# Cross-attention with layer norm on one core: a V projection and a Q projection of the next batch trade steps, and one V projection of the last batch moves an iteration forward

## The chip, the cores and the metric

One Trainium2 chip, of which the kernel uses one core. The metric is device time in microseconds (us). The kernel before took 638.55 us (median of three runs, 637.2 to 639.08).

## The reference

Eight batches. For each, `x` (224 rows of 512) attends to `ctx` (750 rows of 512) with 16 heads of width 32, in float32:

```python
q = (x @ Wq.T + bq); k = (ctx @ Wk.T + bk); v = (ctx @ Wv.T + bv)      # split into 16 heads of 32
att = softmax(einsum('bhqd,bhkd->bhqk', q, k) / sqrt(32))
out = einsum('bhqk,bhkd->bhqd', att, v)                                # heads side by side again
out = x + (out @ Wo.T + bo)
out = (out - mean(out)) / sqrt(var(out) + 1e-05) * gamma + beta
```

All biases, gamma and beta are non-trivial.

## The kernel before, in words

**Tiles.** The queries are two halves of 112 rows, the keys six tiles of 125 (`KT`), the heads four groups of four (`UNITS`, `HG`). A unit is one group of heads of one batch, so there are 32. Projections and scores run in fp16 with each operand split in a high and a low part. A projection is therefore three products for each of four chunks of 512: twelve matmuls. K tasks (`("K", g, half)`) have 375 columns, Q tasks (`("Q", g)`) 224, V tasks (`("V", i)`) 512.

**Steps.** The program is unrolled over the eight batches. An iteration has 32 steps (`STEPS`), eight for each unit. In step s TensorE (PE) first computes the query-major scores of step s+1 (L626, one head, 112 queries, 750 keys), of which VectorE (DVE) takes the row maximum (L928). A step also has key-major score pieces of the unit before (L650), which ScalarE (ACT) exponentiates into `probsT` (L809); the table `PIECES_IN` says how many before, inside and behind the step's task. The third kind of work is the step's projection task (L610). A scores matmul of step s+1 waits until the row maximum of step s-1 is done, since two score banks alternate.

**Sums and visit.** GpSimd (POOL) sums the exponentials of each head over its keys: `pair_sums` (L1036) and two adds into `head_sums` (L1041, L1044). Heads 0 to 3 of a unit are summed at steps 4, 5 and 7 of one slot of eight steps, and at step 0 of the next. At step 2 of that slot (steps 2, 10, 18, 26) PE makes a visit for that unit: 48 matmuls `attend` (L666) and 8 matmuls `sum_keys` (L692), which wait for `head_sums`. ACT copies the result one step later (L817), DVE inverts it (L935, step 4), scales it (L940, step 5) and writes its low half (L950, step 7).

**Tasks.** `OWN` are tasks of this batch, `NEXT` of the next, `OUTPUT` the output projection of the batch before (steps 17 and 20). Two PSUM banks alternate between the tasks of slots' steps 0, 1, 2, 4, 5, 7, where step 2 is the visit. The task of a step may start when the task two uses before in that order is saved (`user_before`), and behind a visit when ACT has copied it. The saving happens one step later: of K and Q tasks ACT writes the high half, then DVE the low half (L885) after that step's row maximum; of a V task DVE alone copies the bank (L890), ahead of that step's row maximum. So K3 of step 31 (`("K", 3, 0)`) must be saved before Q2 of the next iteration's step 1 can start.

**Norm.** The output of the batch before is scaled with `gamma` on DVE (`times_gamma`, L915) at steps 26 and 29, behind the row maximum and the saving; `beta` is added on POOL (`plus_beta`, L1060) at steps 27 and 30. POOL's own order in the stretch is: head 3 (step 24), beta (27), head 0 (28), head 1 (29), beta (30), head 2 (31). Iteration 0 has no output of a batch before.

**DMA queue.** SyncE (SP) issues all loads, the transposes of the tokens, and `fill_stack`, which copies K and Q of a group into stacks with 16 DMAs. Its order at the end of an iteration: `fill(0)`, both stores, `fill(1)` (which waits for K1 and Q1), the load of `resid`; then the transposes of the next iteration. The second store waits for the second `plus_beta`.

**The last batches.** Iteration 6 leaves out the tasks that `LATE` names, and iteration 7 makes them itself, at the steps in `LATE` (`EARLY` is the rest of `NEXT`).

Of the kernel before, what the change touches and what calls it, by code (L numbers as in the profile page):

```python
# [15 lines left out]
def build(nc, x, ctx_tokens, Wq, bq, Wk, bk, Wv, bv, Wo, bo, gamma, beta, out):  # L16
# [49 lines left out]
    VISIT = 2  # L66
    OWN = {0: ("K", 2, 1), 1: ("Q", 2), 4: ("K", 3, 1), 5: ("V", 3), 7: ("V", 4), 8: ("Q", 3), 9: ("V", 5)}
    NEXT = {12: ("K", 0, 0), 13: ("K", 1, 0), 15: ("V", 0), 16: ("V", 1), 21: ("K", 0, 1), 23: ("K", 1, 1), 24: ("Q", 0),
            25: ("Q", 1), 28: ("V", 2), 29: ("K", 2, 0), 31: ("K", 3, 0)}
    SPLIT = {1: (("ctxT", 0),), 2: (("ctxT", 1), ("ctxT", 2)), 10: (("ctxT", 3), ("ctxT", 4), ("ctxT", 5)),  # L70
             18: (("xT", 0), ("xT", 1))}
    SPLIT_ORDER = [t for s in sorted(SPLIT) for t in SPLIT[s]]
# [3 lines left out]
                    ("xT", 0): ("Q", 3), ("xT", 1): ("Q", 3)}  # L76
    OUTPUT = {17: ("O", 0), 20: ("O", 1)}
    FIRST = {2: ("V", 2), 10: ("W", "o", 1), 17: ("W", "o", 2), 20: ("W", "o", 3)}
    LATE = {12: ("V", 0), 13: ("V", 1), 15: ("V", 2)}
    TASK_BANKS = 2  # L80
    IN_BANKS = (0, 1, 2, 4, 5, 7)
    VISIT_BANK = IN_BANKS.index(VISIT) % TASK_BANKS
    EARLY = {s: t for s, t in NEXT.items() if t not in LATE.values()}
    EARLY_V = [t[1] for t in NEXT.values() if t[0] == "V"]
# [35 lines left out]
    def tasks_of(b):  # L120

        known = isinstance(b, int)
        found = dict(OWN) if not known or b < B else {}
        found.update(NEXT if not known or b < LAST - 1 else EARLY if b == LAST - 1 else LATE if b == LAST else {})
        found.update(OUTPUT if not known or b > 0 else FIRST)
# [981 lines left out]
```

## Time and profile before

| | |
|---|---|
| median of three runs | 638.55 us |
| profiled execution | 640.04 us, of which 637.3 us are the span from first to last instruction |
| granted PE clock, mean | 0.994 |
| PE matmul | 611.6 us busy (96%) |
| DVE | 501.1 us (79%) |
| POOL | 468.0 us (73%) |
| ACT | 352.5 us (55%) |

A unit of the trace is a microsecond from the start of the span. PE's busy time takes each matmul with its whole length in the pipeline. Iterations 1 to 5 have the same length to a few hundredths, 74.0 us, so one of them (iteration 4, whose step 25 starts at 382.97) stands for all.

### The profile page before, as it was taken

Reading aid. Unit: us, or ns where it says so; the run is one execution under the profiler, and the core shown is the slowest. Engines: PE = TensorE matmul, PEld = TensorE weight load, DVE = VectorE, ACT = ScalarE, POOL = GpSimd, SP = SyncE. Lnnn points to the kernel's source line nnn. Section 1 sums busy time; section 2 is a strip of 40 time slices with the busy share of each in tenths; the row PEclk is TensorE's granted clock in tenths of the full one; section 3 lists DMA queues with packets and bytes.
Section 4 is the critical chain, followed back from the end, with each engine's and each line's share of the span. In section 5 each row is a group of like instructions: output and inputs, shape, how many; then the busy total and the mean of one; then the engine's idle time right before and its main releaser. Section 6 shows DMA issues by size and latency. Waiting matters only on the chain.

```text
span 637.3 us, 13655 instructions
## 1 busy us (share of the span) xinstructions
PE 611.6 (96%) x5217; PEld 425.4 (67%) x5217; DVE 501.1 (79%) x680; ACT 352.5 (55%) x673; POOL 468.0 (73%) x459
## 2 busy tenths in 40 slices
PE   8998999999999999999999999999999999899894
PEld 7766677766676676766677676766767666576542
DVE  4677787788797797887787887977878887757885
ACT  4514566556565465664665565664656656444661
POOL 9633677784987589784987759785897869775853
PEclk9999999999999999999999999999999999899998
DMA  9574532562245523754137532564237422421020
GB/s 304 186 183 126 133 78 72 133 145 70 65 110 142 129 63 89 151 127 125 38 86 167 143 77 62 115 147 118 69 88 169 96 62 51 107 69 25 2 59 29
DMA packets 95776, 67.02 MB, mean 105 GB/s; under 512 B 69780, under 2 KB 81760, under 8 KB 95712
## 3 DMA queue, kind: packets, MB, share of 16 engines
q1 hardware_dynamic: 95200, 65.41, 41.2%
q0 software_dynamic: 512, 0.75, 0.5%
q8 instruction: 41, 0.67, 0.4%
q14 instruction: 23, 0.19, 0.1%
HBM read 24.52 MB, written 3.67 MB: 44 GB/s over the span
## 4 chain that ended last, share of the span: by engine, by line
PE 69%; POOL 14%; DVE 12%; issue 3%; DMA 1%; ACT 1%; POOLq 0%; SPq 0%; DVEq 0%; ACTq 0%
PE ps_task L610 34%; PE ps_scores L626 10%; PE ps_scoresT L650 8%; PE ps_task L666 6%; POOL pair_sums L1036 6%; DVE top L928 4%; PE ps_task L564 4%; POOL head_sums L1041 3%; DVE token_parts L905 3%; POOL head_sums L1044 3%; PE ps_scores L610 2%; POOL rstd L1056 2%; PE ps_task L692 2%; DVE attn_sums L935 1%; DMA x_in<-in_x 1%
## 5 line engine op out<-in xcount | busy, mean ns | idle before, releaser
L809 ACT ACTIVATE probsT<-ps_scoresT 125x448 f32<-125x448 f32 x384 | 204.5, 544 | 154.2 <-PE ps_scoresT L650 148.4
L928 DVE TENSOR_REDUCE top<-ps_scores 112x1 f32<-112x750 f32 x256 | 234.2, 927 | 63.8 <-PE ps_scores L626 63.0
L1036 POOL TENSOR_TENSOR pair_sums<-probsT 125x672 f32<-125x672 f32 x122 | 197.8, 1621 | 72.3 <-ACT probsT L809 65.6
L650 PE MATMUL ps_scoresT<-stacks 100*125 100x224 f16 x768 | 135.8, 261 | 1.5 <-ACT probsT L809 1.2
L610 PE MATMUL ps_task<-wvT,ctxT 128*125 128x512 f16 x564 | 135.6, 379 | 0.1
L610 PE MATMUL ps_task<-ctxT,wkT 128*128 128x375 f16 x708 | 130.7, 323 | 0.0
L626 PE MATMUL ps_scores<-stacks 96*112 96x512 f16 (+1 forms) x512 | 125.6, 327 | 4.8 <-DVE top L928 4.0
L650 PEld LDWEIGHTS ps_scoresT<-stacks 100*125 100x125 f16 x768 | 94.5, 137 | 41.2 <-ACT probsT L809 4.9
L1041 POOL TENSOR_TENSOR head_sums<-pair_sums 125x224 f32<-125x224 f32 x122 | 96.6, 792 | 11.4
L610 PEld LDWEIGHTS ps_task<-wvT,ctxT 128*125 128x125 f16 x564 | 73.2, 136 | 33.1 <-DVE parts L885 0.4
L1044 POOL TENSOR_TENSOR head_sums<-head_sums,pair_sums 125x224 f32<-125x224 f32 x122 | 87.3, 715 | 9.6
L610 PEld LDWEIGHTS ps_task<-ctxT,wkT 128*128 128x128 f16 x708 | 68.7, 97 | 30.9
L666 PE MATMUL ps_task<-probsT,v 125*32 125x224 f32 x1488 | 80.3, 357 | 0.0
L626 PEld LDWEIGHTS ps_scores<-stacks 96*112 96x112 f16 x512 | 58.0, 130 | 31.0 <-issue 18.7
L890 DVE COPY v<-ps_task 125x512 f32<-125x512 f32 x47 | 32.5, 692 | 44.6 <-PE ps_task L610 44.6
L666 PEld LDWEIGHTS ps_task<-probsT,v 125*32 125x32 f32 x1488 | 43.9, 110 | 23.8 <-issue 0.8
L905 DVE TENSOR_TENSOR token_parts<-ctx_in,token_parts 128x512 f16<-128x512 f32 (+1 forms) x42 | 49.2, 1210 | 4.2 <-ACT token_parts L793 4.2
L935 DVE RECIPROCAL attn_sums<-attn_sums 128x112 f32<-128x112 f32 x64 | 49.8, 818 | 1.5 <-ACT attn_sums L817 1.5
L781 ACT ACTIVATE parts<-ps_task,bk 128x375 f16<-128x375 f32 x59 | 33.7, 571 | 29.4 <-PE ps_task L610 29.4
L564 PE MATMUL ps_task<-woT,attn_parts 128*112 128x512 f16 x192 | 46.0, 379 | 0.1
L610 PE MATMUL ps_task<-xT,wqT 128*128 128x224 f16 x360 | 42.1, 260 | 1.9 <-DVE parts L885 1.9
L798 ACT ACTIVATE stacks<-ps_scoresT 4x896 f16<-4x896 f32 x32 | 28.9, 904 | 25.7 <-PE ps_scoresT L635 25.2
(103 smaller groups left out, 533.7 us busy)
## 6 DMA issues: line engine op xcount, KB each, us to landing
stacks<-parts SPq DMA_DIRECT2D x248, 60.9 KB, 2.0
ctx_in<-in_ctx SPq DMA_DIRECT2D x8, 768.0 KB, 5.5
stacks<-parts SPq DMA_DIRECT2D x124, 46.9 KB, 2.0
resid<-in_x SPq DMA_DIRECT2D x8, 448.0 KB, 4.1
ctx_in<-in_ctx SPq DMA_DIRECT2D x7, 512.0 KB
out_y<-y SPq DMA_DIRECT2D x16, 224.0 KB, 2.3
x_in<-in_x SPq DMA_DIRECT2D x8, 256.0 KB, 3.1
stacks<-parts SPq DMA_DIRECT2D x124, 14.0 KB, 1.8
```

What stands on the lines that cost most here:

```text
L564: last = nc.tensor.matmul(bank[0:QP, :], attn_parts[:, a, k, QP * q:QP * q + QP], wT["o"][:, c, k, :], start=(k == 0 and (a, c) == (0, 0)) ...
L610: last = nc.tensor.matmul(dst, lhsT, rhs, start=first, stop=(n_mm == 0))
L626: last = nc.tensor.matmul(ps_scores[0:QP, s % RING, keys], stacks[0:STACK_ROWS, g, h, NK + QP * q:NK + QP * q + QP], stacks[0:STACK_ROWS, ...
L650: last = nc.tensor.matmul(ps_scoresT[0:KP, piece % 2, NQ * i:NQ * i + NQ], stacks[:, g, h, KP * k:KP * k + KP], stacks[:, g, h, Qc], start ...
L666: last = nc.tensor.matmul(ps_attn[c:c + DK, 0:NQ], v[of_batch][0:KP, k, P * g + c:P * g + c + DK], probsT[0:KP, g % 2, h, k, :], start=(k ...
L809: nc.scalar.activation(probsT[0:KP, g % 2, h, 2 * j:2 * j + 2, :].rearrange("p k q -> p (k q)"), ps_scoresT[0:KP, piece % 2, 0:2 * NQ], AC ...
L905: nc.vector.tensor_tensor(token_parts[rows_in, slot, 1], tokens_in(t, batch)[rows_in], token_parts[rows_in, slot, 0], ALU.subtract).then_i ...
L928: nc.vector.tensor_reduce(top[0:QP, g % 2, HG * q + h:HG * q + h + 1], ps_scores[0:QP, s % RING, 0:NK], AX.X, ALU.max).then_inc(top_ready, 1)
L935: nc.vector.reciprocal(recip[:, cols], recip[:, cols]).then_inc(recip_ready, 1)
L1036: nc.gpsimd.tensor_tensor(pair_sums[0:KP], probsT[0:KP, g % 2, h, 0:3, :], probsT[0:KP, g % 2, h, 3:6, :], ALU.add).then_inc(pair_sums_rea ...
L1041: nc.gpsimd.tensor_tensor(head_sums[0:KP, g % 2, h, :], pair_sums[0:KP, 0], pair_sums[0:KP, 1], ALU.add).then_inc(two_sums_ready, 1)
L1044: nc.gpsimd.tensor_tensor(head_sums[0:KP, g % 2, h, :], head_sums[0:KP, g % 2, h, :], pair_sums[0:KP, 2], ALU.add).then_inc(head_sums_read ...
```

## The change

The tasks of steps 25 and 28 trade places: V2 of the next batch is now made at step 25, ahead of the visit of step 26, and Q1 of the next batch at step 28. `LATE` loses V2: it is made in iteration 6 at step 25 as in any other, and iteration 7 makes V0 at step 13 and V1 at step 15, with nothing at step 12. All other orders stay, and follow from the tables.

```diff
     NEXT = {12: ("K", 0, 0), 13: ("K", 1, 0), 15: ("V", 0), 16: ("V", 1), 21: ("K", 0, 1), 23: ("K", 1, 1), 24: ("Q", 0),
-            25: ("Q", 1), 28: ("V", 2), 29: ("K", 2, 0), 31: ("K", 3, 0)}
+            25: ("V", 2), 28: ("Q", 1), 29: ("K", 2, 0), 31: ("K", 3, 0)}
...
-    LATE = {12: ("V", 0), 13: ("V", 1), 15: ("V", 2)}
+    LATE = {13: ("V", 0), 15: ("V", 1)}
```

## Rows read from the trace of the kernel before

**Rows 1.** The waits of PE: who, for whom, us, times, longest

```profile
PE ps_task L692 <- POOL head_sums L1044: 5.3, 6, 0.9
```

**Rows 2.** Timeline of PE, iteration 4 from step 25: start, us, instruction, idle before

```profile
382.97 0.48 PE L626 MATMUL ps_scores<-stacks 96*112 96x512 f16 x2
384.88 0.48 PE L626 MATMUL ps_scores<-stacks 96*112 96x512 f16 x2
...
388.86 0.59 PE L692 MATMUL ps_task<-head_sums,ones 125*32 125x224 f32 x8 [0.89 <-POOL head_sums L1044]
389.38 0.53 PE L626 MATMUL ps_scores<-stacks 96*112 96x512 f16 x2
...
389.94 0.48 PE L626 MATMUL ps_scores<-stacks 96*112 96x512 f16 x2
...
393.24 0.48 PE L626 MATMUL ps_scores<-stacks 96*112 96x512 f16 x2
...
401.96 0.74 PE L610 MATMUL ps_task<-xT,wqT 128*128 128x224 f16 x6
```

**Rows 3.** Timeline of PE, iteration 4, the visit of step 10, behind V5

```profile
348.35 0.48 PE L626 MATMUL ps_scores<-stacks 96*112 96x512 f16 x2
...
351.74 0.53 PE L626 MATMUL ps_scores<-stacks 96*112 96x512 f16 x2
```

**Rows 4.** Timeline of DVE, iteration 4: step 10, step 18, then steps 26 to 32

```profile
348.35 0.69 DVE L890 COPY v<-ps_task 125x512 f32<-125x512 f32 x1 [1.49 <-PE ps_task L610]
348.96 0.93 DVE L928 TENSOR_REDUCE top<-ps_scores 112x1 f32<-112x750 f32 x1
...
370.77 1.27 DVE L905 TENSOR_TENSOR token_parts<-x_in,token_parts 128x512 f16<-128x512 f32 x2
...
386.62 0.93 DVE L915 SCALAR_TENSOR_TENSOR y<-y,rstd,gamma_row 112x512 f32<-112x512 f32 x1
...
398.79 1.11 DVE L950 SCALAR_TENSOR_TENSOR attn_parts<-attn_sums,bv,attn_parts 128x224 f16<-128x224 f32 x1
...
400.68 0.60 DVE L885 SCALAR_TENSOR_TENSOR parts<-ps_task,bk,parts 128x375 f16<-128x375 f32 x1
```

**Rows 5.** Timeline of POOL, iteration 4, steps 26 to 31

```profile
385.37 1.63 POOL L1036 TENSOR_TENSOR pair_sums<-probsT 125x672 f32<-125x672 f32 x1
387.08 0.99 POOL L1041 TENSOR_TENSOR head_sums<-pair_sums 125x224 f32<-125x224 f32 x1
388.15 0.65 POOL L1044 TENSOR_TENSOR head_sums<-head_sums,pair_sums 125x224 f32<-125x224 f32 x1
...
398.05 1.61 POOL L1036 TENSOR_TENSOR pair_sums<-probsT 125x672 f32<-125x672 f32 x1
```

**Rows 6.** Stretches, step 25 to the next step 2's end: iteration 4, iteration 6

```profile
core 0: us, PE busy (x) PEld busy (x) DVE busy (x) ACT busy (x) POOL busy (x), PEclk, DMA share, GB/s
382.97:406.89 23.92, 23.03 (x238) 16.20 (x236) 18.94 (x26) 13.72 (x28) 21.61 (x21) 1.00 0.28 73
527.41:553.00 25.59, 22.71 (x227) 15.18 (x225) 18.40 (x23) 12.37 (x25) 23.11 (x23) 0.93 0.28 73
```

**Rows 7.** Timeline of PE, iteration 6, step 28 (no task), then iteration 7, step 1

```profile
534.35 0.48 PE L626 MATMUL ps_scores<-stacks 96*112 96x512 f16 x2
...
535.44 0.50 PE L626 MATMUL ps_scores<-stacks 96*112 96x512 f16 x2
...
546.44 0.75 PE L610 MATMUL ps_task<-xT,wqT 128*128 128x224 f16 x6 [1.85 <-DVE parts L885]
```

**Rows 8.** Timeline of DVE, iteration 6, step 29

```profile
537.53 0.88 DVE L928 TENSOR_REDUCE top<-ps_scores 112x1 f32<-112x750 f32 x1
538.32 0.38 DVE L940 TENSOR_TENSOR attn_sums<-attn_sums 128x224 f32<-128x224 f32 x1
```

**Rows 9.** Timeline of POOL, iteration 6, step 29

```profile
537.70 2.47 POOL L1036 TENSOR_TENSOR pair_sums<-probsT 125x672 f32<-125x672 f32 x1
```

**Rows 10.** Timeline of SP, iteration 4, the two stores

```profile
395.62 2.83 SPq L446 DMA_DIRECT2D out_y<-y  x2
```

## The prediction

> **What bounds the kernel now.** I read the page first: PE is busy nearly all the time, so the end is set by PE's work and by its few waits. The waits of PE come next. Apart from start-up and tail they hold one entry that repeats: L692, the key sums of a visit, waits for POOL's `head_sums` six times for 5.3 us in all [rows 1], once in each of iterations 1 to 6. The timeline of PE shows it at step 26. The other visits have none: step 10 stands behind V5 and lasts 351.74 - 348.35 = 3.39 us [rows 3]. Step 26 stands behind Q1 and lasts 389.38 - 384.88 = 4.50 us [rows 2]. The visit thus loses 1.11 us, of which 0.89 are recorded as idle. A second place is the turn from iteration 6 to 7: PE waits 1.85 us there for L885, the low half of K3 (546.44, [rows 7]), and over that stretch the granted clock is 0.93, against 1.00 in the same stretch of iteration 4 [rows 6]. It is full on either side of a part at 1.2 GHz right behind the wait.
>
> **Part 1: the trade of steps 25 and 28, iterations 1 to 6.** A step with a V task lasts 393.24 - 389.94 = 3.30 us, one with a Q task 384.88 - 382.97 = 1.91 us [rows 2]: 1.39 apart. PE's own work stays the same, so without waits the gain would be the 1.11 us of the visit. What hides the wait for POOL is 1.39 us more of matmuls ahead of it. Three queues decide how much is left.
>
> *POOL, before the visit.* Head 3's three adds take 385.37 to 388.80 [rows 5]. They don't depend on step 25's task. But DVE's order in step 26 changes. Now it is row maximum, Q1's low half, L915. In the changed kernel it is V2's copy, row maximum, L915. V2 ends with step 25, at 382.97 + 3.30 = 386.27. As behind V5, the copy starts with the next step and lasts 0.69, and the row maximum starts 0.61 behind it and lasts 0.93 [rows 4]: 386.27, 386.88, end 387.81. L915 then follows at once.
>
> DVE's ops with two operands in SBUF and POOL's adds hold each other up. L1041, from 387.08, lasts 0.99, and ends 0.52 behind L915's end at 387.55; L915 itself had to wait for L1036's end at 387.00 and ended 0.55 behind it [rows 4, 5]. An undisturbed add of that size is L1044 with 0.65 [rows 5]. An undisturbed op of DVE's like L915 takes about 0.6 (two in 1.27, 370.77 [rows 4]). Who is first is settled while DVE still runs the instruction in front. In iteration 6 L1036 started at 537.70, during a row maximum begun at 537.53, and had to wait for L940, which ran only from 538.32; it took 2.47 instead of 1.6 [rows 8, 9]. So a POOL add begun 0.17 us behind the start of a row maximum lost to the op behind it. In the changed kernel that distance is 387.08 - 386.88 = 0.20 us, just as close. I therefore take it that L915 goes first: 387.81 to 388.41, L1041 ends at 388.93, L1044 (0.08 gap, 0.65) at 389.66. PE gets to L692 at 386.27 + 3.39 - 0.52 = 389.14 (0.52 is 389.38 - 388.86 [rows 2]), so 0.6 us of the wait stay. Step 27 starts at 389.66 + 0.06 + 0.52 = 390.24, or 0.86 later than now, and step 28 being 1.39 shorter, step 29 starts 0.53 earlier.
>
> The Trainium skill, in "SBUF — State Buffer", section "Who interferes with whom", says the same more sharply: a DVE instruction with two SBUF inputs contends with a GpSimd instruction that reads SBUF, and whoever issues first holds the port pair for the whole instruction. By that rule the change is worth less than PE's timeline promises; had the two only shared bandwidth, L1041 would end at about 387.8 and the visit would lose nothing. The rows above agree with the rule.
>
> *DVE and POOL, behind the visit.* POOL goes on with beta, two heads, beta and head 2, almost without idle time: L1036 of head 2 ends at 399.66, 10.86 us behind `head_sums` [rows 5]. L950 on DVE waits for it (398.79, 1.11 long, ends 0.24 behind it), then comes a row maximum, then the low half of K3, which ends at 401.28 [rows 4]. Q2 on PE starts at 401.96 [rows 2]. So this chain now has 0.68 us of slack, which is all that PE can gain before it waits for L885 instead. In the forecast POOL's pass starts 0.86 later. It would end at 400.52, K3 be saved at 402.14, and Q2 start at 402.20, 0.24 later than now. Some of DVE's interference in the pass may fall away, since L940 (the scaling) and L915 of step 29 now come while L1036 of head 1 runs; I take half of that difference and Q2 at 402.1. The trade is then worth about -0.15 us for each of six iterations: the gain at the visit is given back at step 1 as a new wait of about 0.7 us. -0.25 and +0.2 are its bounds while L915 goes first. Iteration 0 has neither the wait nor L915 or the betas: nothing.
>
> Other costs of the move are hidden. ACT loses the high half of Q1 in step 26 and gets it in step 29, where it has idle time. Q1's low half (0.44) comes to DVE in step 29 in place of V2's copy (0.69), so DVE isn't later for it. Q1 is saved about 3 us later than now, and SP's `fill(1)` with its 16 DMAs waits for it; but it also stands behind the second store, whose issue ends at 398.45 [rows 10], 3 us or so behind Q1's new saving, so neither the fill nor what is queued on SP behind it (the load of `resid`, the next transposes) is moved by the trade. A later beta moves that store by up to 0.9 us; the stacks it fills are read at step 7 first. The wait at L610 of step 31 for Q1's low half is over some 1 us before.
>
> **Part 2: V2 goes from iteration 7 to iteration 6.** Now iteration 6 has no task in step 28, which lasts 535.44 - 534.35 = 1.09 us [rows 7]. The stretch from step 25 to the end of the next step 2 takes 25.59 us although it has 2.2 us less of matmuls than that of iteration 4, with 23.92 us [rows 6]. The short step sends PE ahead of DVE, and the wait and the half clock behind it cost 25.59 - (23.92 - 2.21) = 3.9 us. Changed, the stretch is as in other iterations: 25.59 - 23.92 = 1.67 us gained. In iteration 7 step 12 has no task: 3.30 becomes 1.09, 2.21 us gained. PE is the last there, and DVE and POOL have idle time from step 9 to step 24, so I count it whole; a new wait there could take all of it (bounds 0 and 2.21). Sum of part 2: 3.88 us.
>
> **Sum.** 3.88 - 6 x 0.15 = 2.98 us, taken as 3.0. The profiled execution of 640.04 us (span 637.3 and 2.7 around it) would become 637.0, with a span of 634.3. It is 1.5 above the median, from which I subtract the same: 638.55 - 3.0 = 635.5 us.
>
> **The rivals.** *B: POOL goes first.* L1041 starts 0.2 us into the row maximum and may get through, as the distance is so small. Then it ends at 387.74, L1044 waits for L915 and ends at 388.93, the wait at the visit is gone, and the pass starts 0.13 later than now. K3 is saved at about 401.4 at most, less the interference that falls away 401.25, and Q2 starts at 401.4: 0.55 us gained in each of six. 3.88 + 3.3 = 7.2: 631.4 us. If nothing bound at step 1, 3.88 + 6 x 1.11 = 10.5 us, 628.0; the slack of 0.68 speaks against it.
>
> *C: slower.* The wait at Q2 in step 1 grows until the clock falls. That is what iteration 6 shows: L940 took the port ahead of L1036, POOL's pass ran 0.86 longer, PE waited 1.85 us, and the episode cost 3.9 us. Should each of six iterations get it, the loss is 6 x (3.9 - 1.1) = 16.8 us less 3.9: about 651 us. For it: PE comes 0.5 us earlier to step 29. Against it: with Q1's low half between the row maximum and L940, L1036 of head 1 starts 0.7 us ahead of L940's turn. It decides from the point where the pass ends more than about 1 us later than forecast.
>
> *D: nothing much.* Step 12's 2.21 us turn into a wait elsewhere in iteration 7, and the trade loses 0.15 or 0.2 in six iterations: 1.67 - 1.0 = 0.7 us, 637.9 us.
>
> **Chances.** Forecast 0.50, B 0.27, D 0.14, C 0.09. A measurement of this kernel can tell about 0.3% from no change, 1.9 us. Forecast and B are faster (0.77), D is within (0.14), C is slower (0.09). The range holds forecast, B and most of D: 630.0 to 638.3 us.
>
> **What would show it.** In the profile after: step 25 3.3 us long and step 28 1.9; L1041 behind step 25 about 1.8 us long and L692 still waiting, 0.5 to 0.6 us (forecast), or L1041 0.66 and no wait (B); at step 1 a wait of Q2 for L885 of 0.4 to 0.8 us in iterations 2 to 7; no wait of 1.85 us at the start of iteration 7 and a granted clock of 1.00 there; step 12 of iteration 7 about 1.1 us. The prediction is wrong if Q2 doesn't wait at all, or if the clock falls in iterations 2 to 6.

## The result, and the profile after

| | before | changed |
|---|---|---|
| median beside each other | 638.62 us | 632.88 us |
| ratio, 95% interval | | 0.9911 (0.9892 to 0.993) |
| profiled execution (span) | 640.04 us (637.3) | 632.54 us (630.7) |
| the pair once more, in another job | 638.33 us | 634.09 us, ratio 0.994 (0.9926 to 0.9954) |

The kernel became faster, by 5.7 us in the first comparison (4.5 to 6.9) and 4.2 us in the second. The forecast was 3.0 us. Two executions with a low granted clock are left out of all times and ratios here (902.32 us of the kernel "POOL 1.1 us later" at 0.655, and 651.95 us of the kernel before at 0.944).

Reading the trace after goes in the order of the prediction. First the waits of PE:

```profile
PE ps_scores L626 <- DVE top L928: 4.0, 5, 1.5
PE ps_task L610 <- DVE parts L885: 2.8, 6, 0.5
```

The entry of [rows 1], L692 waiting for POOL, is gone altogether. L610 now waits for the low half of K3 six times, 0.45 to 0.5 us each, where it waited once for 1.85 us before. The timeline of PE in iteration 4 (step 25 starts 1.31 us earlier than before) answers to [rows 2]:

```profile
381.66 0.49 PE L626 MATMUL ps_scores<-stacks 96*112 96x512 f16 x2
...
385.05 0.48 PE L626 MATMUL ps_scores<-stacks 96*112 96x512 f16 x2
...
387.95 0.56 PE L692 MATMUL ps_task<-head_sums,ones 125*32 125x224 f32 x8
388.45 0.53 PE L626 MATMUL ps_scores<-stacks 96*112 96x512 f16 x2
...
389.01 0.48 PE L626 MATMUL ps_scores<-stacks 96*112 96x512 f16 x2
...
390.87 0.48 PE L626 MATMUL ps_scores<-stacks 96*112 96x512 f16 x2
...
399.27 0.49 PE L626 MATMUL ps_scores<-stacks 96*112 96x512 f16 x2
400.21 0.75 PE L610 MATMUL ps_task<-xT,wqT 128*128 128x224 f16 x6 [0.45 <-DVE parts L885]
```

Step 25 lasts 3.39 us, the visit of step 26 3.40 (4.50 before), step 28 1.86. The visit has lost all but 0.01 of its extra 1.11 us. At step 1 Q2 starts 0.94 us behind the step's start (401.96 - 401.63 = 0.33 before). The timelines of DVE and then of POOL in the same stretch answer to [rows 4, 5]:

```profile
385.06 0.69 DVE L890 COPY v<-ps_task 125x512 f32<-125x512 f32 x1 [1.58 <-PE ps_task L610]
385.67 0.93 DVE L928 TENSOR_REDUCE top<-ps_scores 112x1 f32<-112x750 f32 x1
386.51 1.19 DVE L915 SCALAR_TENSOR_TENSOR y<-y,rstd,gamma_row 112x512 f32<-112x512 f32 x1
...
397.35 1.43 DVE L950 SCALAR_TENSOR_TENSOR attn_parts<-attn_sums,bv,attn_parts 128x224 f16<-128x224 f32 x1
...
399.55 0.60 DVE L885 SCALAR_TENSOR_TENSOR parts<-ps_task,bk,parts 128x375 f16<-128x375 f32 x1
```

```profile
384.05 1.60 POOL L1036 TENSOR_TENSOR pair_sums<-probsT 125x672 f32<-125x672 f32 x1
385.74 0.67 POOL L1041 TENSOR_TENSOR head_sums<-pair_sums 125x224 f32<-125x224 f32 x1
386.49 0.66 POOL L1044 TENSOR_TENSOR head_sums<-head_sums,pair_sums 125x224 f32<-125x224 f32 x1
387.78 1.27 POOL L1060 TENSOR_TENSOR y<-y,beta_row 112x512 f32<-112x512 f32 x1 [0.63 <-DVE y L915]
...
396.92 1.61 POOL L1036 TENSOR_TENSOR pair_sums<-probsT 125x672 f32<-125x672 f32 x1
```

POOL went first. L1041 starts 0.07 us into the row maximum and is through 0.19 us before its end. L1044 starts 0.11 us before that end. Both run at full speed (0.67 and 0.66 us), and L915 waits for L1044 (1.19 us long, its end is 0.55 behind L1044's). Between L1044 and L915 it is a near tie, since their recorded starts are 386.49 and 386.51, and no more than 0.03 us apart in any of iterations 1 to 6. The sums are ready at 387.15, 0.8 us before PE comes for them. Then POOL itself waits 0.63 us, because beta needs L915. Its pass (beta, two heads, beta and L1036 of head 2) ends at 398.53, L950 0.25 behind it, the low half of K3 is saved at 400.15, and Q2 starts at 400.21. From the end of L1036 to K3's saving it is 1.62 us, as before.

Last, the stretch from step 25 to the next step 2's end, iteration 4 and iteration 6 ([rows 6]; columns as there):

```profile
381.66:405.15 23.49, 23.04 (x238) 16.27 (x236) 19.62 (x26) 13.91 (x28) 21.28 (x21) 1.00 0.28 71
525.23:548.72 23.49, 23.04 (x238) 16.27 (x236) 18.03 (x24) 12.49 (x25) 21.18 (x21) 1.00 0.29 74
```

Each is 0.43 us shorter than iteration 4's 23.92 before, and iteration 6's is 2.10 shorter than its own 25.59, without a part at 1.2 GHz. Step 12 of iteration 7, from one scores matmul to the next on PE, lasts 1.09 us, 2.2 less:

```profile
568.17 0.48 PE L626 MATMUL ps_scores<-stacks 96*112 96x512 f16 x2
...
569.26 0.50 PE L626 MATMUL ps_scores<-stacks 96*112 96x512 f16 x2
```

In spans 6.6 us are gone: 6 x 0.43, 1.67 of iteration 6's old turn, and 2.21, which is 6.46, and 0.1 of start-up.

### The profile page after: what moved, and what is told of

Read it like the earlier page. It is cut to its first block, busy times and chain, and to the rows that moved or that the text cites. A ratio compares the mean times of both kernels' runs of the same rounds, so it can differ in the third digit from the quotient of the medians.

```text
span 630.7 us, 13655 instructions
## 1 busy us (share of the span) xinstructions
PE 609.9 (97%) x5217; PEld 425.7 (67%) x5217; DVE 503.4 (80%) x680; ACT 353.6 (56%) x673; POOL 465.7 (74%) x459
## 4 chain that ended last, share of the span: by engine, by line
PE 80%; DVE 17%; issue 1%; ACT 1%; POOL 0%; POOLq 0%; ACTq 0%; DVEq 0%
PE ps_task L610 35%; PE ps_task L666 11%; PE ps_scores L626 11%; PE ps_scoresT L650 9%; DVE top L928 7%; PE ps_task L564 7%; PE ps_scores L610 2%; DVE attn_sums L935 2%; DVE parts L885 2%; DVE attn_parts L950 2%; PE ps_task L692 2%; DVE token_parts L905 2%; DVE y L915 1%; DVE attn_sums L940 1%; PE ps_scores L678 1%
## 5 line engine op out<-in xcount | busy, mean ns | idle before, releaser
L928 DVE TENSOR_REDUCE top<-ps_scores 112x1 f32<-112x750 f32 x256 | 233.2, 923 | 45.1 <-PE ps_scores L626 44.3
L1036 POOL TENSOR_TENSOR pair_sums<-probsT 125x672 f32<-125x672 f32 x122 | 196.8, 1613 | 64.8 <-ACT probsT L809 57.1
L610 PE MATMUL ps_task<-wvT,ctxT 128*125 128x512 f16 x564 | 135.9, 379 | 0.1
L610 PE MATMUL ps_task<-ctxT,wkT 128*128 128x375 f16 x708 | 130.7, 323 | 0.0
L626 PE MATMUL ps_scores<-stacks 96*112 96x512 f16 (+1 forms) x512 | 125.2, 326 | 4.7 <-DVE top L928 4.0
L1041 POOL TENSOR_TENSOR head_sums<-pair_sums 125x224 f32<-125x224 f32 x122 | 92.8, 761 | 11.4
L610 PEld LDWEIGHTS ps_task<-wvT,ctxT 128*125 128x125 f16 x564 | 73.0, 136 | 34.9 <-DVE parts L885 2.2
L1044 POOL TENSOR_TENSOR head_sums<-head_sums,pair_sums 125x224 f32<-125x224 f32 x122 | 89.3, 732 | 9.6
L610 PEld LDWEIGHTS ps_task<-ctxT,wkT 128*128 128x128 f16 x708 | 68.8, 97 | 30.9
L626 PEld LDWEIGHTS ps_scores<-stacks 96*112 96x112 f16 x512 | 57.7, 130 | 29.5 <-issue 18.7
L610 PE MATMUL ps_task<-xT,wqT 128*128 128x224 f16 x360 | 41.8, 259 | 2.8 <-DVE parts L885 2.8
```

The source lines that it names most:

```text
L610: last = nc.tensor.matmul(dst, lhsT, rhs, start=first, stop=(n_mm == 0))
L626: last = nc.tensor.matmul(ps_scores[0:QP, s % RING, keys], stacks[0:STACK_ROWS, g, h, NK + QP * q:NK + QP * q + QP], stacks[0:STACK_ROWS, ...
L928: nc.vector.tensor_reduce(top[0:QP, g % 2, HG * q + h:HG * q + h + 1], ps_scores[0:QP, s % RING, 0:NK], AX.X, ALU.max).then_inc(top_ready, 1)
L1036: nc.gpsimd.tensor_tensor(pair_sums[0:KP], probsT[0:KP, g % 2, h, 0:3, :], probsT[0:KP, g % 2, h, 3:6, :], ALU.add).then_inc(pair_sums_rea ...
L1041: nc.gpsimd.tensor_tensor(head_sums[0:KP, g % 2, h, :], pair_sums[0:KP, 0], pair_sums[0:KP, 1], ALU.add).then_inc(two_sums_ready, 1)
L1044: nc.gpsimd.tensor_tensor(head_sums[0:KP, g % 2, h, :], head_sums[0:KP, g % 2, h, :], pair_sums[0:KP, 2], ALU.add).then_inc(head_sums_read ...
```

## The experiments

This table has the times from one iteration's first scores matmul (L626 in step 0, which computes the scores of step 1) to the next's, worked out from each trace. Iteration 2 is within 0.07 us of iterations 3 to 5. The column of iteration 7 runs to the end of the span.

| us | it. 0 | it. 1 | its. 3 to 5, each | it. 6 | it. 7 | ratio to before, interval |
|---|---|---|---|---|---|---|
| before | 67.1 | 74.07 | 74.03 | 68.40 | 95.70 | |
| changed | 67.1 | 72.98 | 73.60 | 69.98 | 90.32 | 0.9911 (0.9892 to 0.993) |
| swap only | 67.1 | 72.98 | 73.6 | 69.59 | 92.62 | 0.9957 (0.9942 to 0.9972) |
| last batch only | 67.1 | 74.07 | 74.04 | 70.42 | 89.70 | 0.9975 (0.9962 to 0.9987) |
| two memsets on POOL | 67.1 | 72.98 | 73.62 | 69.98 | 91.4 | 0.9929 (0.9912 to 0.9945) |
| six memsets on POOL | 67.1 | 72.97 | 73.6 | 69.99 | 90.4 | 0.9925 (0.9902 to 0.9948) |
| POOL 0.5 us later | 67.1 | 72.97 | 73.60 | 69.97 | 91.70 | 0.9949 (0.9931 to 0.9967) |
| POOL 1.1 us later | 67.1 | 73.62 | 74.3 | 70.68 | 92.38 | 1.001 (0.9996 to 1.0024) |
| changed, low half later | 68.8 | 72.97 | 72.97 | 69.35 | 89.70 | 0.9872 (0.9852 to 0.9892) |
| before, low half later | 68.8 | 74.07 | 74.03 | 68.42 | 92.67 | 0.9972 (0.9955 to 0.9989) |
| changed, once more | 67.1 | 72.98 | 73.61 | 69.99 | 90.4 | 0.994 (0.9926 to 0.9954) |
| changed, low half later, once more | 67.1 | 72.97 | 72.98 | 69.36 | 89.7 | 0.9863 (0.985 to 0.9877) |

The 68.8 of iteration 0 goes with a part at 1.2 GHz (last section). So does part of the column of iteration 7.

### The trade alone

```diff
-    LATE = {13: ("V", 0), 15: ("V", 1)}
+    LATE = {12: ("V", 0), 13: ("V", 1), 15: ("V", 2)}
```

> The trade of steps 25 and 28 alone; the last batch's three V projections stay in its own iteration, so iteration 6 has no task at step 25 and Q1 at step 28. Theory (the trade is worth 1.1 us of visit wait less what comes back at step 1, and the rest of the change's gain lies in iterations 6 and 7): iterations 1 to 5 as in the changed kernel, 0.43 us each shorter than before, 2.2 in all; in iteration 6 PE reaches the visit 2.2 us early and waits there some 1.5 to 2 us, and Q2 of iteration 7 still waits. Time 634.5 to 636.5 us. Rival (the trade carries nearly all of the gain, part 2 little): 633 us or less.

Measured 635.69 us against 638.16. The loop is that of the changed kernel. In iteration 6, which has no task in step 25, PE reaches the visit early and waits for POOL there once. Beside six entries for L885, the waits of PE have:

```profile
PE ps_task L692 <- POOL head_sums L1044: 1.5, 1, 1.5
```

But the long wait at the start of iteration 7 is short here too (0.53 us), since Q1 now fills step 28. Iterations 6 and 7 together take 162.2 us, 1.9 less than before without any V projection having left iteration 7. The measured time lies in the theory's range, and above the rival's 633 us.

### The last batch alone

```diff
-    LATE = {12: ("V", 0), 13: ("V", 1), 15: ("V", 2)}
+    LATE = {13: ("V", 0), 15: ("V", 1)}
```

(in the kernel before)

> Only the last batch's V2 is moved: it is made in iteration 6 at step 28, with the order of the kernel before in the loop, and iteration 7 makes V0 and V1 at steps 13 and 15. Theory: the stretch from step 25 of iteration 6 to the end of step 2 of iteration 7 takes 23.9 us, not 25.6, with no wait of 1.85 us and no part at 1.2 GHz, and step 12 of iteration 7 takes 1.1 us, not 3.3: 3.9 us gained, 634.7 us. Rival (two parts that need each other): under 2 us gained.

The trace gives what was expected. The loop is unchanged, as its waits of PE show:

```profile
PE ps_task L692 <- POOL head_sums L1044: 5.4, 6, 0.9
```

and iterations 6 and 7 take 160.1 us, 4.0 less than before. (The span is only 3.1 us shorter, since the first scores come 0.78 us later in this trace, at 36.37 for 35.59.) The measured time doesn't give it: 637.12 against 638.16 us, by the ratio 1.6 us (0.8 to 2.4), which is the rival's "under 2 us" and not the theory's 3.9. The rival's reason, that the parts need each other, isn't borne out: by their ratios the two parts alone give 2.7 and 1.6 us, together 4.3, and the change gave 4.2 to 5.7. Part of the difference lies in the kernel before. Its profiled execution had a mean clock of 0.994 and a span of 637.3 us; of the 18 others measured beside this run 13 had 0.996 and spans of 635.3 to 636.7. The part at 1.2 GHz behind the wait of iteration 7, some 1.7 us of loss, is thus most likely not there in most executions. Where the clock fell in those can't be seen, since only one was traced. Ten of the twelve executions of this kernel, too, had a lower mean clock (0.992 to 0.995) than its profiled one (0.996), so some of the shortfall may be on its side. By this estimate part 2 is worth about 2 us in most executions and 4 in the traced one. The two parts also overlap: in the traces they give 4.0 and 1.9 us in iterations 6 and 7 singly, and 3.8 together, because both take away the same wait of 1.85 us.

### Which goes first, L915 or POOL's adds

```diff
+                    if s == 3 * UNIT and 0 < b < B:
+                        for i in range(2):
+                            nc.gpsimd.memset(idle[:, 2 * (b - 1) + i], 0.0)
                     for back, i, h in SUM_STEPS:
```

> The changed kernel with two memsets of one column on POOL (some 0.09 us each) ahead of head 3's adds in step 24 of iterations 1 to 7: L1041 then starts some 0.25 us into DVE's row maximum of step 26 instead of 0.07. Theory of the prediction (a DVE op asks for the port while the row maximum in front of it runs, so who comes first is decided in the first 0.1 to 0.2 us of it): L915 goes first, L1041 lasts about 1.7 us, L692 waits 0.5 us, 3 to 4 us slower than the changed kernel. Rival (L915 asks only when its turn has come): POOL's L1041 stays at 0.66 us and nothing waits at the visit; L1044 now comes behind L915; the time is that of the changed kernel within 1 us.

> The changed kernel with six memsets of one column on POOL (0.06 us each) ahead of head 3's adds in step 24 of iterations 1 to 7: L1041 starts some 0.33 us into DVE's row maximum of step 26 (0.07 in the changed kernel, 0.09 with two memsets, which moved it too little). Early asking (a DVE op asks for the port while the row maximum in front of it runs): L915 goes first, L1041 lasts 1.4 to 1.6 us, L692 waits 0.4 us and the betas come 0.6 us later, so Q2's wait at step 1 grows by 0.6 us: 3 to 4 us slower than the changed kernel's 632.9. Late asking (L915 asks when its turn comes): L1041 0.66 us, L915 between L1041 and L1044, no wait at the visit, Q2's wait within 0.2 us of 0.45, time within 1 us.

Neither moved L1041 as it should. The six memsets took 0.25 us together and part of it went into a gap that was there, so L1041 began 0.09 and 0.08 us into the row maximum. L1041 kept its 0.67 us, nothing waited at the visit, and the times were 634.17 and 633.68 us. So these runs don't decide between early and late asking. They have one thing to show, in iteration 1 of the kernel with six memsets (line numbers are one higher in the kernels with an addition on POOL: L916 is L915, L929 is L928, L1042 and L1045 are L1041 and L1044):

```profile
165.87 0.74 DVE L916 SCALAR_TENSOR_TENSOR y<-y,rstd,gamma_row 112x512 f32<-112x512 f32 x1
```

```profile
165.90 1.23 POOL L1045 TENSOR_TENSOR head_sums<-head_sums,pair_sums 125x224 f32<-125x224 f32 x1
```

Here the near tie went the other way: L1045 came 0.03 us behind L916's start and took 1.23 us for 0.66. The iteration still has 72.97 us, so who wins that tie costs nothing.

So I put one power operation in their place, and then two:

```diff
+                    if s == 3 * UNIT and 0 < b < B:
+                        for i in range(1):      # 2 in the other kernel
+                            nc.gpsimd.tensor_tensor(idle[0:QP, i:i + 1], eps[0:QP], minus_half[0:QP], ALU.pow)
```

> The changed kernel with one small power op on POOL (some 0.5 us) ahead of head 3's adds in step 24, since the memsets of the two runs before cost too little to move them: L1041 starts 0.5 to 0.6 us into DVE's row maximum of step 26, whose successor is L915. Early asking: L915 goes first, L1041 lasts 1.2 us or more. Late asking: L1041 keeps 0.66 us, L915 runs between it and L1044, and L1044 lasts about 1 us; head 3's sums are then ready 0.5 to 0.8 us later than in the changed kernel, at the limit of what makes L692 wait (0 to 0.2 us).

With one, 634.4 us. DVE, then POOL, iteration 4:

```profile
385.66 0.93 DVE L929 TENSOR_REDUCE top<-ps_scores 112x1 f32<-112x750 f32 x1
386.51 0.77 DVE L916 SCALAR_TENSOR_TENSOR y<-y,rstd,gamma_row 112x512 f32<-112x512 f32 x1
```

```profile
386.07 0.66 POOL L1042 TENSOR_TENSOR head_sums<-pair_sums 125x224 f32<-125x224 f32 x1
386.81 0.99 POOL L1045 TENSOR_TENSOR head_sums<-head_sums,pair_sums 125x224 f32<-125x224 f32 x1
```

L1042 starts 0.41 us into the row maximum, twice the distance at which the prediction had it lose, and runs at full speed. L916's turn comes at 386.59, while L1042 runs; it goes next, ahead of L1045, which ends 0.52 behind it. So in this place the gamma op asks when its turn comes. The iteration is not a hundredth longer, since beta now starts right behind L1045, where it had waited for L915 before. Half a microsecond of POOL's time is free at this place. A loss against the changed kernel isn't shown: that one took 632.88 us and, once more, 634.09. The trace has 1.4 us more in iteration 7 (91.70 for 90.32). The longest wait for a row maximum there is 1.60 us for 1.31, and behind it stands a part at 1.2 GHz that the trace of the changed kernel doesn't have (columns as in [rows 6]):

```profile
599.90:606.70 6.80, 6.62 (x49) 3.28 (x49) 6.80 (x5) 3.74 (x8) 6.28 (x7) 0.51 0.11 34
```

> The changed kernel with two small power ops on POOL (some 0.55 us each) ahead of head 3's adds in step 24: L1041 comes some 0.2 us behind the moment at which L915 can run, so L915 must go first by either theory. This makes the forecast's case on the chip: L1041 lasts about 1.1 us, L692 waits 0.4 to 0.7 us at the visit, the pass of POOL behind it starts 0.6 us later and Q2's wait at step 1 grows by about as much less the wait at the visit. Whole trade then worth about nothing for each iteration: 3 to 4 us slower than the changed kernel, 636 to 637 us. Rival (the pass of POOL has slack, Q2's wait is not tied to it): at most the 0.5 us of the visit are lost and nothing of Q2's wait changes.

With two, 639.44 us, the forecast's case:

```profile
388.32 0.74 DVE L916 SCALAR_TENSOR_TENSOR y<-y,rstd,gamma_row 112x512 f32<-112x512 f32 x1
```

```profile
388.43 1.17 POOL L1042 TENSOR_TENSOR head_sums<-pair_sums 125x224 f32<-125x224 f32 x1
```

```profile
390.38 0.59 PE L693 MATMUL ps_task<-head_sums,ones 125*32 125x224 f32 x8 [0.43 <-POOL head_sums L1045]
...
402.72 0.46 PE L611 MATMUL ps_task<-xT,wqT 128*128 128x224 f16 x3 [0.51 <-DVE parts L886]
```

L1042 comes 0.11 us behind L916's start and waits for it (1.17 us long), and PE waits 0.43 us at the visit, which lasts 4.03 us for 3.40. Against step 25's start POOL's pass begins 0.69 us later than in the changed kernel. PE itself is 0.63 us later by the visit, so Q2's wait grows by no more than 0.06, from 0.45 to 0.51 us. That is what was expected: a wait at the visit, and at step 1 the delay of the pass less what PE has lost already. The rival, a pass with slack, is excluded: L951 (L950 here) ends 0.25 us behind the pass's last L1037 again (401.30 and 401.05), so with slack in the pass PE's delay would have taken Q2's wait away. An iteration takes 74.3 us, 0.27 more than before the change. The forecast for this case was 0.15 more.

Iterations 1 to 6 are 4.1 us longer than in the changed kernel, and 3 to 4 were expected for the whole. What comes on top is in iteration 7, 2.1 us longer. The two operations stand ahead of the last sums there, and PE waits 2.18 us for a row maximum, not 1.31, which is 0.9 of it. The rest comes behind the next wait (1.32 us), where the granted clock is 0.57 from 609 to 613.

### The low half of step 31 behind the saving of K3

```diff
-                    for u, g_u in due("low", b, s):
+                    for u, g_u in due("low", b, s) if s < STEPS - 1 else []:
+                        attn_low(u, g_u)
+                    for u, g_u in due("low", b - 1, STEPS - 1) if s == 0 and b > 0 else []:
                         attn_low(u, g_u)
```

> The changed kernel, where DVE writes the low half of the attention of step 31 (L950) only in the next iteration's step 0, behind the saving of K3. Theory (what PE waits for at step 1 is POOL's L1036 of head 2, by way of L950 on DVE and the port they share): Q2's wait of 0.45 us at step 1 goes, step 1 lasts 1.87 instead of 2.49 us in iterations 2 to 7, 3.7 us gained, 629.2 us. Rival (K3's low half is late by the row maxima of DVE alone): the wait stays, no change within 1 us.

Measured 630.48 us, for 629.2 expected. The waits of PE have no line for L610 at all. DVE, iteration 4:

```profile
396.48 1.77 DVE L928 TENSOR_REDUCE top<-ps_scores 112x1 f32<-112x750 f32 x2
398.17 0.59 DVE L885 SCALAR_TENSOR_TENSOR parts<-ps_task,bk,parts 128x375 f16<-128x375 f32 x1
398.68 0.80 DVE L950 SCALAR_TENSOR_TENSOR attn_parts<-attn_sums,bv,attn_parts 128x224 f16<-128x224 f32 x1
```

The two row maxima now stand together and K3 is saved at 398.76 instead of 400.15. All iterations from 1 to 5 take 72.97 us, and PE waits for nothing in them. The theory's 3.7 us are there from iteration 2 on. The 1.3 us that lack in the time go with iteration 0, which is 1.7 us longer in this trace (last section), and three of the four executions have the mean clock of the traced one, 0.993. The run shows that L950's place ahead of K3's saving makes Q2 wait. That L950 is long because it waits for POOL's L1036 is read from the trace of the changed kernel: it takes 1.43 us at 397.35 and ends 0.25 behind L1036, and takes 0.43 at 380.02, with none of these adds beside it. No run has L950 in its old place without that add.

> The changed kernel once more, on the same chip and beside the next one. Expected: 632.9 us, iterations 2 to 5 of 73.60 us with Q2 waiting 0.45 us at step 1.

> The changed kernel with L950 of step 31 moved behind the saving of K3 once more. Expected if the wait at step 1 is gone for good: iterations 2 to 6 shorter by 0.63 us each and the start of iteration 7 as well, 3.8 us under the changed kernel, 629.1 us; up to 1.7 us of it is taken back in executions in which the clock falls to 1.2 GHz behind the 1.5 us wait in iteration 0, as in the first run of it. Rival (the gain is the clock's and chance's): no more than 1.5 us under the changed kernel.

The pair on one chip: 634.09 us, ratio 0.994 (0.9926 to 0.9954), and 629.38 us, ratio 0.9863 (0.985 to 0.9877). This version is faster than the changed kernel by 4.7 us, where 3.8 were expected, and is the fastest here. The rival, at most 1.5 us, is excluded.

The same edit in the kernel before:

> The kernel before, where DVE writes the low half of the attention of step 31 only in the next iteration's step 0, behind the saving of K3. Theory (L950, held up by POOL's L1060 and L1036, is what made K3 late at the turn to iteration 7): the wait of 1.85 us there goes or falls under 0.3 us, and with it any part at 1.2 GHz behind it; the other iterations, with 0.68 us of slack at that place, don't change. 2 us faster than before (636 us). Rival (PE, ahead by an empty step 28, runs into DVE's queue whatever its order): the wait stays above 1 us.

Measured 636.84 against 638.58 us. PE at the start of iteration 7:

```profile
546.09 0.74 PE L610 MATMUL ps_task<-xT,wqT 128*128 128x224 f16 x6
...
551.24 0.58 PE L692 MATMUL ps_task<-head_sums,ones 125*32 125x224 f32 x8 [0.52 <-POOL head_sums L1046]
```

Q2's wait of 1.85 us is gone, and 0.5 us come back at the next visit. The other iterations stay at 74.03. So that wait needed L950's place in DVE's order. It needed PE's lead as well, for in the kernel with the last batch's move alone, where step 28 has its task, it is gone with L950 in its old place.

## Why the prediction was right or wrong

**Right in direction, 2.7 us short in size** in the first comparison, 1.2 in the second. The mechanism of the trade was the one of rival B (0.27), not that of the forecast (0.50). By its steps:

- *The wait at the visit is worth 1.11 us, and a V task ahead of it covers it.* Right; visit and step lengths came as read from rows.
- *"I therefore take it that L915 goes first."* This step failed. One precedent, [rows 8, 9], was taken for a rule. In the changed kernel and the experiments L915 never held up an add that had started 0.07, 0.08, 0.09 or 0.41 us into the row maximum (nor one at 0.67, in iteration 6 of the trade alone); it did so only with adds that came 0.03 and 0.11 us behind its own start. The distance came out smaller too, 0.07 for 0.20 us: step 25 took 3.39 instead of 3.30, because V2 (382.02) starts just behind the saving of K1 (381.97), and POOL was 0.03 earlier. The trade gave 0.43 us an iteration instead of -0.15: 3.5 us over six. That is rival B, in its mechanism and nearly in its size (0.55).
- *Behind the visit the gain is bound by POOL's pass, L950, and K3's low half.* Right. The two power operations show that Q2's wait follows the pass, and the experiment with L950 that L950 carries it to K3. One link was missing: beta also waits for L915, so when POOL goes first, its pass still starts only when L915 is done. It starts 6.12 us behind step 25's start, 5.79 before, which is 0.33 later where B had 0.13. Since B's time for Q2 was rounded up by some 0.1, of these 0.2 us 0.12 are left between B's 0.55 and 0.43.
- *Part 2 is worth 3.88 us.* Right for the traced execution. As a term of the median it was too large, since alone it measured 1.6 us (0.8 to 2.4). Up to 1.7 us of it was time at 1.2 GHz that one execution had and most others, by their mean clock, probably didn't have. There was a sign of it in the prediction's own numbers: the profiled execution was 1.5 us above the median, and the prediction carried this 1.5 over to the kernel after unchanged. This error and that of L915 have opposite signs: 3.0 + 3.5 - 1.7 = 4.8, between the two measurements. That they partly cancel is luck. With L915 first as forecast and part 2 at its measured 1.6 us, the gain would have been an estimated 1.6 - 0.9 = 0.7 us, rival D's size.
- *C*, a growing wait with a falling clock, didn't come, nor did *D*: step 12 gave its whole 2.2 us.

## What to carry to other kernels

When a task is moved to cover a wait, look for the next engine queue whose order has slack of the same size; here 1.11 us were won at one place and 0.6 paid at the next, and a change of DVE's order by one operation there was worth about as much as the whole change. Work that no one needs soon (L950) must not stand ahead of a result that PE waits for, above all if it can be held up by another engine. And a part at a low clock in the one profiled execution is to be checked against the clock and span of the other executions before it goes into a sum.

## What the runs showed of the hardware

Behind waits of PE of 1.3 to 2.2 us the granted clock fell to 1.2 GHz in some traces and not in others. In iteration 0 PE waits 1.47 or 1.48 us for a row maximum in every trace. First the changed kernel, then the one with the low half later, in the stretch of 10 us around it (columns as in [rows 6]):

```profile
60.00:70.00 10.00, 8.27 (x52) 5.60 (x53) 8.10 (x11) 5.26 (x11) 7.60 (x9) 1.00 0.74 189
```

```profile
60.00:70.00 10.00, 8.05 (x42) 5.26 (x43) 7.64 (x11) 4.93 (x10) 6.24 (x6) 0.83 0.74 184
```

The mean of 0.83 is a loss of 1.7 us in 10, which is the 68.8 against 67.1 us in the table. Iteration 7 of the kernel before lost the same behind its wait of 1.85 us. Near the end of iteration 7 PE waits for a row maximum twice, 1.30 to 1.33 us each. In the kernels with power operations the first of these waits is 1.60 us (one operation, with no second wait) or 2.18 us (two). Behind these waits the clock fell in three traces: two memsets (0.57 from 605.9 to 609.9), one power operation (above) and two (0.57 from 609 to 613). In the others it didn't. From iteration 0 to PE's last matmul no wait of 0.9 us or less was followed by it in any trace.

When a DVE instruction that stands behind another one is in time to hold up POOL isn't told by one rule here. The gamma op goes by its turn (0.41 us into the row maximum L1042 still ran at full speed). The scaling in [rows 8, 9] held up an add that began 0.6 us before the scaling ran, and the same two instructions did so again in the trace of the kernel before with the low half later (L1038 from 539.35, 2.48 us; L940 from 539.98). The Trainium skill ("SBUF — State Buffer", "Who interferes with whom") has it that whoever issues first gets the shared port pair for the whole instruction. The traces agree where both starts are seen: L1042, 0.11 us behind the gamma op's start, took 1.17 us for 0.66. Why the gamma op and the scaling differ (in the kernel the gamma op stands behind three semaphore waits, the scaling behind one) is open.
